# A convolution in sixteen tiles of the array, and the loop over quads written out

## The reference

```python
x = x + window_attention(layernorm(shift(x)));  x = x + mlp(layernorm(x))      # layer 0: 7x7 windows, 3 heads
h = layernorm(x) @ w_in[:, :48] + b_in[:48]                                    # layer 1
x = x + silu(conv3x3(h, conv_w, padding='SAME') + conv_b)
for l in (2, 3):                                                               # layers 2 and 3
    x = x + fourier_mixer_l(layernorm(x));  x = x + float8_ffn_l(layernorm(x))
```

## Time and profile before

| what | value |
|---|---|
| median of 3 runs | 4319.72 us (4318.26 to 4321.03) |
| the profiled execution's own time | 4321.37 us |
| its span, first to last instruction | 4319.7 us, 131667 instructions |
| PE / ACT / DVE busy | 3681.6 / 1843.0 / 1767.9 us |
| mean granted clock of PE | 0.938 |

### The profile page before, as it was taken

The page is one execution under the profiler, slowest core; times in us unless marked ns, Lnnn a source line. Parts: engine busy times, 40 slices in busy tenths (PEclk is TensorE's granted clock), DMA queues, the critical chain, the costliest instruction groups (busy, mean ns, idle before and its releaser), DMA issues.

```text
span 4319.7 us, 131667 instructions
## 1 busy us (share of the span) xinstructions
PE 3681.6 (85%) x55580; PEld 2510.3 (58%) x55580; DVE 1767.9 (41%) x2885; ACT 1843.0 (43%) x3483; POOL 232.0 (5%) x489
## 2 busy tenths in 40 slices
PE   3988879988798888988889979889788897899887
PEld 2647646467455674556745647546566475564755
DVE  3523454234543345334353344533445234452344
ACT  1453444433454334444345444453443534435344
POOL 3400000000000000000000000000000000000000
PEclk7999999999899999899999999899999999999989
DMA  4201001010010100101001010010100101001000
GB/s 120 51 22 27 2 14 27 16 27 3 14 27 16 26 3 14 27 16 27 3 14 41 2 26 3 15 41 2 26 3 15 40 2 26 12 6 25 18 11 13
DMA packets 24223, 88.72 MB, mean 21 GB/s; under 512 B 17843, under 2 KB 18211, under 8 KB 19643
## 3 DMA queue, kind: packets, MB, share of 16 engines
q1 hardware_dynamic: 22339, 74.72, 7.2%
q0 software_dynamic: 1280, 5.21, 0.4%
HBM read 63.86 MB, written 14.84 MB: 18 GB/s over the span
## 4 chain that ended last, share of the span: by engine, by line
PE 74%; ACT 8%; DVE 6%; issue 6%; SPq 3%; DMA 2%; ACTq 0%; DVEq 0%
PE ps L986 74%; ACT rs L605 3%; ACT lv L600 3%; DVE area_ty L822 2%; DMA area_ty<-area_hz 2%; SPq L429 1%; SPq L412 1%; DVE xs L955 1%; ACT sq L592 1%; DVE area_hz L843 0%; DVE area_ty L927 0%; DVE area_hz L925 0%; DVE area_ty L951 0%; ACT area_ty L646 0%; ACT area_ty L650 0%
## 5 line engine op out<-in xcount | busy, mean ns | idle before, releaser
L822 DVE TENSOR_TENSOR area_ty<-ps,rs 128x448 f32<-128x448 f32 (+2 forms) x416 | 285.1, 685 | 633.1 <-ACT rs L605 633.1
L986 PE MATMUL ps<-area_hz 32*64 32x147 f32 (+2 forms) x7180 | 376.8, 296 | 84.2 <-DVE area_hz L843 31.3
L986 PE MATMUL ps<-area_ty,area_hz 113*64 113x49 f32 (+1 forms) x10240 | 403.4, 253 | 44.8 <-DMA area_ty<-area_hz 41.1
L703 ACT ACTIVATE area_ty<-ps 120x448 f32<-120x448 f32 (+1 forms) x448 | 243.8, 544 | 450.7 <-PE ps L986 450.7
L927 DVE COPY area_ty<-ps 120x448 f32<-120x448 f32 (+1 forms) x432 | 270.0, 625 | 399.5 <-PE ps L986 399.5
L703 ACT ACTIVATE area_hz<-ps 112x384 f32<-112x384 f32 (+2 forms) x384 | 191.4, 498 | 531.6 <-PE ps L986 531.6
L986 PEld LDWEIGHTS ps<-area_ty,area_hz 113*64 113x64 f32 (+1 forms) x10240 | 339.5, 137 | 122.2 <-issue 119.3
L986 PE MATMUL ps<-sq,keep_sb 128*128 128x448 f32 (+1 forms) x832 | 382.4, 562 | 26.7 <-ACT sq L592 26.6
L986 PEld LDWEIGHTS ps<-area_hz 32*64 32x64 f32 (+2 forms) x7180 | 297.0, 160 | 181.3 <-issue 152.5
L986 PE MATMUL ps<-area_ty,wconv 128*128 128x448 f32 x1008 | 398.0, 539 | 0.1
L986 PE MATMUL ps<-keep_sb,area_hz 112*56 112x56 f32 (+1 forms) x12288 | 367.7, 222 | 14.7 <-DVE area_hz L925 13.8
(11 more groups left out here) (106 smaller groups left out, 4219.0 us busy)
## 6 DMA issues: line engine op xcount, KB each, us to landing
area_hz<-f_all SPq DMA_DIRECT2D x16, 2541.0 KB
xw<-x_in SPq DMA_DIRECT2D x8, 1568.0 KB, 6.8
y_out<-xs SPq DMA_DIRECT2D x32, 294.0 KB
f_all<-piece POOLq DMA_DIRECT2D x16, 317.6 KB, 3.4
area_ty<-area_hz SPq DMA_DIRECT2D x256, 4.6 KB
area_hz<-raw_in SPq DMA_DIRECT2D x1, 2894.0 KB, 9.3
g_sb<-g_in SPq DMA_DIRECT2D x2, 1396.5 KB
g_sb<-g_in SPq DMA_DIRECT2D x1, 1470.0 KB
```

The lines of the kernel that those rows point to most:

```text
L703: act.activation(dst, src, ACT.Relu if st in (ST_H, ST_F2) else ACT.Copy).then_inc(sc_kept, 1)
L822: ve.tensor_tensor(o, a, b, ALU.mult, **kw).then_inc(normed, 1)
L986: return pe.matmul(o, a, b, start=start, stop=stop)
```

## The change

`conv` is written anew, and the loops over quads are replaced by Python loops, so that all eight quads stand one after another in each engine's program and waits are on constants. The mixer's code has no line in the diff.

- The image is two halves (`GROUPS`) of 28 rows; a half is four chunks of 7 rows (392 pixels). A `tap` of a half is 16 matmuls of 32 x 32 weights: image j (rows 32j of the array) and chunk c (columns 32c) write partitions 32c of bank 4g + j. `wconv` holds the 32 x 32 matrices alone.
- SiLU works on a half in two pieces of two banks (784 pixels a partition), in place in `yc`, which now lies in `area_y`.
- The result lies by chunk and not by image, so `move` puts it right with 16 matmuls by the identity, and DVE adds from PSUM to `xs`, chunk by chunk.
- All seven norms of the convolution come before those of the mixer; centers use banks 4 to 6 (three ahead), variances bank 7. Mixer tiles 0 to 2 follow the first half, 3 to 6 the second, in banks 0 and 1 (centers) and 2 and 3 (variances).

```diff
+GROUPS, GROUP_ROWS = 2, HW // 2
+CHUNKS = 4
+CR = GROUP_ROWS // CHUNKS
+CW = CR * HW
+LAST_OF = [3, NT - 1]
+MIX_OF = [(0, 3), (3, NT)]
@@ _tile_order @@
-    for s in range(CONV_SLOTS):
-        order += [(w, i) for w, i in ((LN_CONV, s + 2), (LN_MIX(0), s - 1)) if 0 <= i < NT]
+    order += [(LN_CONV, i) for i in range(2, NT)] + [(LN_MIX(0), i) for i in range(NT)]
@@ every engine @@
-            with pe.Fori(0, nq) as q:
+            for q in range(nq):
@@ scalar: conv @@
+                for i in range(NT):
+                    if i + 1 < NT:
+                        square(q, LN_CONV, i + 1)
+                    invert(q, LN_CONV, i)
+                for g in range(GROUPS):
+                    k = (q * GROUPS + g) * 2
+                    act.wait_ge(conved, q * GROUPS + g + 1)
+                    for p in range(2):
+                        act.activation(yc[:, g, 2 * p:2 * p + 2, :],
+                                       ps[:, 4 * g + 2 * p:4 * g + 2 * p + 2, 0:CW], ACT.Exp, scale=-1.0,
+                                       bias=act_bias[:, 0:1]).then_inc(neg_exped, 1)
...
+                    first, end = MIX_OF[g]
+                    square(q, LN_MIX(0), first)
+                    for i in range(first, end):
+                        if i + 1 < end:
+                            square(q, LN_MIX(0), i + 1)
+                        invert(q, LN_MIX(0), i)
@@ vector: conv @@
+                for i in range(NT):
+                    scale_conv(q, i)
+                for g in range(GROUPS):
+                    for p in range(2):
...
+                        ve.scalar_tensor_tensor(o, ps[:, 4 * g + 2 * p:4 * g + 2 * p + 2, 0:CW], K("cb"), o,
                                                 ALU.add, ALU.mult).then_inc(silued, 1)
+                    for c in range(CHUNKS):
...
+                        ve.tensor_tensor(xs[:, sl], xs[:, sl], ps[:, 4 * g + c, 0:CW], ALU.add
+                                         ).then_inc(conv_added, 1)
+                    for i in range(*MIX_OF[g]):
+                        scale_mix(q, 0, i)
@@ tensor: conv @@
+                def tap(g, n):
+                    dy, dx = n // 3, n % 3
+                    pe.sem_inc(passed_pe, 1)
+                    for c in range(CHUNKS):
+                        h = GROUP_ROWS * g + CR * c + dy
+                        for j in range(QI):
+                            r = slice(RW * j, RW * j + RW)
+                            ins = mm(ps[RW * c:RW * c + RW, 4 * g + j, 0:CW].rearrange("p (h w) -> p h w", w=HW),
+                                     wconv[r, n, :], pad[r, h:h + CR, dx:dx + HW], start=n == 0, stop=n == 8)
                     return ins
+                def move(g):
+                    pe.wait_ge(silued, (q * GROUPS + g + 1) * 2)
+                    pe.sem_inc(passed_pe, 1)
+                    for c in range(CHUNKS):
+                        r = slice(RW * c, RW * c + RW)
+                        for j in range(QI):
+                            ins = mm(ps[RW * j:RW * j + RW, 4 * g + c, 0:CW], ident[r, r], yc[r, g, j, :])
+                        ins.then_inc(conv_moved, 1)
...
                 center_conv(0)
                 center_conv(1)
+                pe.wait_ge(mlp_added, q * NW + NW)
+                center_conv(2)
                 variance(q, LN_CONV, 0)
+                for i in range(3, 6):
+                    variance(q, LN_CONV, i - 2)
+                    center_conv(i)
+                variance(q, LN_CONV, 4)
                 pe.wait_ge(border, q + 1)
+                pe.wait_ge(normed, ln_count(q, LN_AT[LN_CONV, LAST_OF[0]]))
+                tap(0, 0)
+                center_conv(6)
+                tap(0, 1)
+                variance(q, LN_CONV, 5)
+                tap(0, 2)
+                variance(q, LN_CONV, 6)
+                for n in range(3, 9):
+                    ins = tap(0, n)
+                ins.then_inc(conved, 1)
+                pe.wait_ge(normed, ln_count(q, LN_AT[LN_CONV, LAST_OF[1]]))
+                for n in range(6):
+                    tap(1, n)
+                move(0)
+                tap(1, 6)
+                center_mix(0)
+                tap(1, 7)
+                center_mix(1)
+                variance_mix(0)
+                tap(1, 8).then_inc(conved, 1)
+                center_mix(2)
+                variance_mix(1)
+                variance_mix(2)
+                move(1)
+                center_mix(3)
+                center_mix(4)
+                for i in range(3, NT):
+                    variance_mix(i)
+                    if i + 2 < NT:
+                        center_mix(i + 2)
```

More of the change, by code:

```diff
@@ L85, in LN_FFN @@
     return 4 + 2 * l
-CONV_SLOTS = NT + 1
+GROUPS, GROUP_ROWS = 2, HW // 2
[4 more added lines that the diff above has]
+MIX_OF = [(0, 3), (3, NT)]
 FFN_SLOTS = NT + 3
@@ L135, in center_bank @@
     if which == LN_CONV:
+        return 4 + i % 3
+    if which == LN_MIX(0):
         return i % 2
-    return {LN_MIX(0): 4, LN_MIX(1): 1, LN_WIN1: 1}.get(which, 0)
+    return {LN_MIX(1): 1, LN_WIN1: 1}.get(which, 0)
 def variance_bank(k):
     which, i = LN_ORDER[k] if k >= 0 else (LN_FIRST, k + NW)
-    if which in (LN_FIRST, LN_WIN2, LN_CONV):
+    if which in (LN_FIRST, LN_WIN2, LN_MIX(0)):
         return 2 + i % 2
-    return {LN_MIX(0): 5, LN_MIX(1): 3, LN_WIN1: 3}.get(which, 2)
+    if which == LN_CONV:
+        return 7
+    return {LN_MIX(1): 3, LN_WIN1: 3}.get(which, 2)
 def user_before(bank, k):
@@ L238, in build_kernel @@
         w2 = sb("w2", [HID, RW])
-        wconv = sb("wconv", [128, 9, QI, RW])
+        wconv = sb("wconv", [128, 9, RW])
         mix1 = sb("mix1", [128, 2, QI * CI])
@@ L298, in build_kernel @@
         pad = area_t[:, 0:PADW * PADW].rearrange("p (h w) -> p h w", w=PADW)
[L299 to L303, removed]
+        yc = area_y.rearrange("p (g j n) -> p g j n", g=GROUPS, j=QI)
         h1 = area_h[:, 0:CI * 120].rearrange("p (s w) -> p s w", w=120)
@@ L344, in build_kernel @@
             sem("mlp_up"), sem("gelu_done"), sem("mlp_down"), sem("mlp_added"), sem("tile_reordered"))
-        border, conved, neg_exped, log1ped, sigmoided, silued, conv_added = (
+        border, conved, neg_exped, log1ped, sigmoided, silued, conv_moved, conv_added = (
             sem("border_zeroed"), sem("conv_made"), sem("conv_negative_exp"), sem("conv_log"),
-            sem("conv_sigmoid"), sem("silu_done"), sem("conv_added"))
+            sem("conv_sigmoid"), sem("silu_done"), sem("silu_at_its_image"), sem("conv_added"))
         terms_loaded, table_made, table_stored = (
@@ L361, in build_kernel @@
         passed_pe, passed_ve, passed_gp = sem("pe_passed"), sem("vector_passed"), sem("gpsimd_passed")
-        N_WIN, N_SETUP_VE = 33, 37
+        N_WIN, N_SETUP_VE = 33, 34
         block = ctx.enter_context(nc.Block())
@@ L442, in tables @@
                 load_table(q, 1)
-            with sp.Fori(0, nq - 1) as q:
+            for q in range(nq - 1):
                 write_max_rows(q)
@@ L515, in middle_pads @@
                 ins.then_inc(pads_ready, 1)
-            with gp.Fori(0, nq) as q:
+            for q in range(nq):
                 gp.wait_ge(attended, q * NW + NW)
@@ L671, in conv @@
                 square(q, LN_CONV, 0)
[L672 to L685, removed]
-                                       bias=act_bias[:, 0:1]).then_inc(neg_exped, 1)
[L687 to L694, removed]
@@ new lines, in conv @@
+                for i in range(NT):
[8 more added lines that the diff above has]
+                                       ps[:, 4 * g + 2 * p:4 * g + 2 * p + 2, 0:CW], ACT.Exp, scale=-1.0,
+                                       bias=act_bias[:, 0:1]).then_inc(neg_exped, 1)
+                    for p in range(2):
+                        o = yc[:, g, 2 * p:2 * p + 2, :]
+                        act.wait_ge(neg_exped, k + p + 1)
+                        act.activation(o, o, ACT.Ln, bias=act_bias[:, 1:2]).then_inc(log1ped, 1)
+                    for p in range(2):
+                        o = yc[:, g, 2 * p:2 * p + 2, :]
+                        act.wait_ge(log1ped, k + p + 1)
+                        act.activation(o, o, ACT.Exp, scale=-1.0).then_inc(sigmoided, 1)
+                    first, end = MIX_OF[g]
[4 more added lines that the diff above has]
+                        invert(q, LN_MIX(0), i)
@@ L737, in _ @@
             norm(0, LN_FIRST)
-            with act.Fori(0, nq) as q:
+            for q in range(nq):
                 window_attention(q)
@@ L805, in _ @@
             ve.wait_ge(su_pe, 6)
[L806 to L809, removed]
+            su(ve.tensor_copy(wconv[:, :, :], ps[:, 5, 0:9 * RW].rearrange("p (t n) -> p t n", t=9)))
             assert n_su[0] == N_SETUP_VE, n_su[0]
@@ L900, in conv @@
             def conv(q):
[L901 to L908, removed]
+                for i in range(NT):
+                    scale_conv(q, i)
+                for g in range(GROUPS):
+                    for p in range(2):
```

(32 more changed lines are left out.)

## The result

The changed kernel takes 4157.33 us (median of 4, 4145.97 to 4166.33) against 4320.38 us: ratio 0.9622, 95% interval 0.9601 to 0.9643. The forecast was 4166 us, with a range of 4110 to 4240. The profiled execution took 4159.9 us; its span is 161.6 us shorter than before.

A forecast was written before the change was run, and what follows sets the result against it. PE, busy 85% of the span, was taken to bound the kernel. From 4321.4 us, 126 for the convolution stages and 28 for the loops came off, giving 4167, or 4166 for the median; 8-in-10 range 4110 to 4240.

The forecast's parts named there:

- Taps: Convolution stage: 16 tiles at once, 0.70 us a tap; 18 taps take 12.6 us instead of 47.3.
- Lead: Start of the convolution stage: first tap at 10.9 instead of 5.7 us, as tiles 0 to 3 need norms.
- New wait: Convolution stage, ACT: SiLU of half 1 starts 5.6 us late, behind mix tiles 0 to 2.
- Tail: End of convolution stage: rounds of 4.0 us through two center banks, plus 60% of a 5.8 us slow-clock cost.
- Stage: Whole convolution stage: 63.7 us instead of 79.5; 15.8 us gained, times 8: 126 us.
- Jumps: Seven quad ends: straight code removes PE's pieces without a wait, 28 us gained.
- Registers: Register arithmetic before waits: its removal costed at nothing, bounds 0 and 10 us.
- Stalls: PE stalls without a semaphore during table transfers, five pieces, 26.9 us: no change taken.
- Rival (a): Sparse convolution tail at full clock, or table stalls gone: stage 60.2 us, total 4111 us; chance 0.15.
- (b): Taps limited by instruction delivery, weight loads or eight at a time: 1.3 us each, total 4230; chance 0.16.
- (c): Taps run only four matmuls at once: 2.6 us a tap, total 4432 us; chance 0.07.
- (d): Loop gain lost: quad ends wait as long and every table stalls PE; total 4218 us; chance 0.12.

The follow-up runs named there:

- 5: Changed kernel with the two loops of a tap exchanged (`for j` outside, `for c` inside); single run 4155.67 us.
- experiment 11: Changed kernel with tail-bank, filler and later-table edits, plus SiLU of half 1 before finishing mixer tiles 1 and 2, banks 4 to 7, five fillers; 4006.63 us.
- 3: Changed kernel with the centers of mixer tiles 5 and 6 in banks 5 and 4 instead of 1 and 0; 4087.79 us, ratio 0.9466.
- 4: Changed kernel with nine extra matmuls, result unused, while PE waits before the second move; 4131.24 us, ratio 0.9575.
- 9: Changed kernel with the second table's load issued after the first ffn's first tile, not before the inverse transform's last stage; 4115.77 us, ratio 0.9526.
- experiment 2: Changed kernel with its loops over quads put back, nothing else; 4219.97 us, ratio 0.9767 against the kernel before.

## Why the prediction was right, point by point

- **Taps.** Sixteen tiles do run at once. A tap was priced at 0.70 us: the first of a run takes 0.68, the later ones 0.84 (changed kernel, confirmed by 5). The prediction set the weight loads' price below the stream's; with 32 passes in a row 0.18 us come on top, cause open. Mis-sized: about 2 us a stage, 1.4 of it in half 0 (done at 21.7 us, 20.3 forecast); the first six taps of half 1 stay hidden beside the SiLU. The 0.99 us that follow from the Trainium skill's 10.6x ("TensorE: Matmul & The Clock Gate", Part 3) were too high. Its floor of 25 ns a pass (0.80 us; it stands in Part 1 of that page) is near by chance: with 168 columns 15 ns a pass were measured.
- **Lead.** It was worked out as 10.9 us and measured as 10.79 to 10.80 in every quad.
- **New wait.** The SiLU is 5.6 us late, as forecast; in experiment 11, with ACT's order changed, the wait is gone.
- **Tail.** The ring through two banks is shown by 3. At full clock the forecast puts 27.5 us from last tap to mixer, and the tails of 4 that kept their clock have 27.6. With the slow clock 31.0 were forecast and 31.0 to 33.5 measured, mean 31.9, so the 60% taken for it was somewhat too small.
- **Stage.** 63.7 forecast, 66.4 measured (530.9/8): 105 us gained instead of 126. Two terms were small: taps (some 1.9 us) and clock (0.9).
- **Jumps.** 28 us were forecast and 31 came: 29 by the piece without a wait, and 2 because at three of the seven ends the first two passes of the new quad run at full clock. The late instruction packets at these ends fit the reason that the prediction gives.
- **Registers.** They were costed at nothing, with bounds of 0 and 10 us, from the dense passes. That step failed: they gave 17 us, at the joins of stages, where a row of 0.48 us "issue" stood in the chain before. The prediction looked for them inside dense work, where they are indeed hidden (10.36 us in both kernels), and not behind a stage's last copy.
- **Stalls.** They were forecast as unchanged and nearly were: the chain before has four of 5.5 to 6.9 us and four of 1.37 us, 31.0 us in all, of which the prediction counted one of the four short ones (26.9). Now they are 24.7 us, and the stage that they stand in takes 91.5 us over the run instead of 100.5. Their cause, a fetch behind the table transfer, was an inference; it is supported by the late packets above and by 9, which moves only that transfer.
- **Sum.** 105 + 31 + 17 = 153 of the span's 161.6 us; the rest is the sum of changes of up to 20 us, of both signs, in the other stages. 154 were forecast: the stage 21 us too good, the loops 20 us too poor, and the others at nothing. That the total is 9 us from the forecast is partly luck, as errors of 20 us cancel.

Rival (a) is refuted by the clock of 0.67 and the stalls, (b) and (c) by taps of 0.84 us, (d) by the quads' ends.

## What to carry to other kernels

Cutting a block-diagonal matmul into 32 x 32 tiles gives back most of the array, and the stage then belongs to whatever ran beside it: here the tail of small dependent steps, where two banks, an engine's fixed order and a slow clock cost more than the taps. Look at a dependent tail's queue for an instruction that waits for a buffer with others behind it; one line for banks gave 69 us, where the whole new convolution gave 96 (experiment 2). Write a loop out where the chain shows "issue" at its end or right behind waits, and keep large transfers away from stretches in which PE takes in many small instructions (4157 to 4116 us in experiment 9).

## What the runs showed that was not expected

- Nine matmuls whose result nobody reads made the kernel 26 us faster (4131.24 against 4157.33), by the clock of the work behind them. Experiment 4 expected it, the prediction did not have it.
- The same 16 tiles take 0.68 us a tap when passes start 7 ns apart and 0.84 when they start 17 ns apart.
- 15 ns a pass with its weight load (32 weight columns, 168 columns) is possible for some 120 passes or more; then PE waits for 0.7 to 2.0 us with no semaphore.
- Runs of straight code spread more: 60 us for loops only, against 15 us for the kernel before on the same chip (4310.69 to 4325.99). That this comes from the number of stalls is a guess, as only one execution of each kernel has a trace.
